# Two stacked graph layers with layer norms: column tiles one step later, and another order of work on VectorE

## The reference

```python
node = x @ W1                                   # x: 4096 x 128, W1: 128 x 16
hw   = einsum('nc,kcf->nkf', x, W2)             # W2: 16 x 128 x 128
x0   = einsum('nk,nkf->nf', node, hw)
h    = relu(adj @ x0 + node @ b)                # adj: 4096 x 4096, fp32
x1   = layernorm(x + h)                         # over the 128 features
msg  = x1 @ W + B
wts  = where(adj < 1, exp(-(1/adj - 1)**2 * 2), 0)
out  = layernorm(x1 + wts @ msg)
```

## Time and profile before

| | |
|---|---|
| median of 3 runs | 615.34 us (614.74 to 616.6) |
| profiled execution: its own time | 615.66 us |
| profiled execution: span | 613.8 us |
| TensorE busy | 570.2 us (93%) |
| ScalarE busy | 511.5 us (83%) |
| VectorE busy | 479.9 us (78%) |
| mean granted clock of TensorE | 0.982 |

### The profile page before, as it was taken

How to read it: one execution, slowest core, us unless ns; L and a number is a source line. 1 busy time by engine, 2 the same in 40 slices (tenths; PEclk the granted TensorE clock), 3 DMA queues, 4 the chain that set the end, 5 groups by cost and what they waited for, 6 DMA issues and landing times.

```text
span 613.8 us, 5199 instructions
## 1 busy us (share of the span) xinstructions
PE 570.2 (93%) x1742; PEld 322.4 (53%) x1742; DVE 479.9 (78%) x539; ACT 511.5 (83%) x542; POOL 90.2 (15%) x78
## 2 busy tenths in 40 slices
PE   6999998796899989998999899999989998988887
PEld 5888886343455545554555455545545554533332
DVE  5677778777478789879987998799789879958752
ACT  4788787859746989898989889898989898988994
POOL 1899998200000000000000000000000000000000
PEclk9999999989799999999999999999999999999989
DMA  4990000687287887787978778777887874453011
GB/s 160 361 375 18 20 0 0 230 338 288 107 304 285 308 312 280 280 321 263 336 271 338 275 280 324 289 287 287 308 310 280 280 301 186 188 205 137 18 52 68
DMA packets 22986, 142.25 MB, mean 232 GB/s; under 512 B 2704, under 2 KB 2864, under 8 KB 6576
## 3 DMA queue, kind: packets, MB, share of 16 engines
q1 hardware_dynamic: 22672, 141.65, 61.8%
q10 hardware_dynamic: 288, 0.27, 0.2%
HBM read 139.81 MB, written 2.10 MB: 231 GB/s over the span
## 4 chain that ended last, share of the span: by engine, by line
PE 53%; ACT 18%; DVE 16%; issue 8%; DMA 3%; POOL 1%; SPq 0%; POOLq 0%; ACTq 0%; DVEq 0%
PE l_ps L369 20%; PE acc_ps L334 8%; DVE wt L601 5%; PE hw_ps L306 5%; PE hw_ps L308 5%; PE hw_ps L307 5%; ACT wt L481 4%; ACT wt L469 3%; ACT wt L474 3%; ACT wt L464 3%; DVE wt L595 3%; DVE adj_lo L588 3%; DVE adj_hi L586 3%; DMA row_in<-adjT_dram 2%; PE acc_ps L327 2%
## 5 line engine op out<-in xcount | busy, mean ns | idle before, releaser
L369 PE MATMUL l_ps<-wt,msg 128*128 128x512 f32 x512 | 232.4, 597 | 12.9 <-DVE msg L632 10.9
L369 PEld LDWEIGHTS l_ps<-wt,msg 128*128 128x128 f32 x512 | 96.6, 191 | 130.9 <-issue 113.1
L595 DVE SCALAR_TENSOR_TENSOR wt<-wt 128x2048 f32<-128x2048 f32 x64 | 148.1, 2313 | 0.0
L464 ACT ACTIVATE wt<-wt 128x2048 f32<-128x2048 f32 x64 | 121.5, 1898 | 21.6 <-DVE wt L595 21.6
L334 PE MATMUL acc_ps<-row_in,x 128*128 128x512 f32 x264 | 123.1, 612 | 3.9 <-DMA row_in<-adjT_dram 3.9
L469 ACT ACTIVATE wt<-wt 128x2048 f32<-128x2048 f32 x64 | 122.4, 1912 | 2.0
L481 ACT ACTIVATE wt<-wt 128x2048 f32<-128x2048 f32 x39 | 74.3, 1905 | 40.7 <-DVE wt L601 40.7
L601 DVE SCALAR_TENSOR_TENSOR wt<-wt 128x2048 f32<-128x2048 f32 x39 | 89.1, 2284 | 8.0 <-ACT wt L469 8.0
L451 ACT ACTIVATE prods<-hw_ps,node 128x128 f32<-128x128 f32 x256 | 73.2, 373 | 18.7 <-PE hw_ps L308 17.5
L334 PEld LDWEIGHTS acc_ps<-row_in,x 128*128 128x128 f32 x264 | 51.7, 197 | 69.1 <-issue 68.9
L568 DVE SCALAR_TENSOR_TENSOR part_acc<-hw_ps,node,part_acc 128x128 f32<-128x128 f32 x224 | 60.7, 342 | 19.8 <-PE hw_ps L308 19.8
(11 more groups left out here) (63 smaller groups left out, 383.0 us busy)
## 6 DMA issues: line engine op xcount, KB each, us to landing
row_in<-adjT_dram SPq DMA_DIRECT2D x64, 1024.0 KB, 6.8
wt<-adjT_dram SPq DMA_DIRECT2D x64, 1024.0 KB, 4.8
x_in<-xT_dram SPq DMA_DIRECT2D x8, 256.0 KB, 3.6
x_row<-xT_dram SPq DMA_DIRECT2D x8, 256.0 KB, 6.1
outT_dram<-sumT SPq DMA_DIRECT2D x8, 256.0 KB, 2.0
W_in<-W_dram SPq DMA_DIRECT2D x3, 256.0 KB, 4.7
W_in<-W_dram ACTq DMA_DIRECT2D x1, 256.0 KB, 4.0
B_sb<-B_dram SPq DMA_DIRECT2D x1, 256.0 KB, 5.2
```

The lines of the kernel that those rows point to most:

```text
L369: mm = pe.matmul(l1_ps[:, t % L1_BANKS, :], msg[:, c % 2, k, :], wt[t % WT_RING][:, k, :], start=(k == 0), stop=(k == CH - 1))
L464: act.activation(w[:, :, :], w[:, :, :], ACT.Ln, bias=TINY).then_inc(ln_made, 1)
L595: dve.scalar_tensor_tensor(out=w, in0=w, scalar=1.0, in1=w, op0=ALU.is_lt, op1=ALU.mult).then_inc(mask_made, 1)
```

## The change

`COL_LAG` goes from 12 to 13: column tile t is worked at step t + 13, and its logarithm, mask, square and sum each move one step with it. `messages`, `copy_messages`, `scale_row` and `add_row` move one place too, while the row's square and inverse root on ScalarE stay. The first six weight tiles' logarithms stand at steps 0, 3, 5, 7, 10, 12 in place of 0, 2, 4, 6, 8, 10. `W1b` is made within block 1 of stage one, in a corner of a bank that the node products use, and copied after `sum_over_k(1)`. Weight tiles 6 and 7 are loaded at steps 3 and 4 of SP's loop. Within a step VectorE does: residual or copy of messages, scale, add, add of the row, square, mask, split; before it was residual or copy, add, split, mask, scale and add of the row, square. The second norm has three banks for its centred values and one for its variances, in place of two and two.

```diff
-COL_LAG = 12
+COL_LAG = 13
-FIRST_EVEN = 6
-LAST_EVEN = 58
-LAST_STEPS = (66, 67, 69, 70, 72, 73)
+FIRST_STEPS = (0, 3, 5, 7, 10, 12)
+FIRST_EVEN = len(FIRST_STEPS)
+LAST_STEPS = (67, 68, 69, 71, 72, 73)
+LAST_EVEN = 64 - len(LAST_STEPS)
...
-            return 2 * m
+            return FIRST_STEPS[m]
...
-        w1b_ps = var_ps[:, 0:P]
+        w1b_ps = acc_ps[:, 1, P:2 * P]
...
-        yc2_ps = [acc_ps[:, j % 2, :] if j < NB - 2 else l1_ps[:, j % 2, :] for j in range(NB)]
-        var2_ps = [yc_ps, var_ps]
+        yc2_ps = [(acc_ps[:, 0, :], acc_ps[:, 1, :], yc_ps[:, :])[j % 3] if j < NB - 2 else l1_ps[:, j % 2, :]
+                  for j in range(NB)]
...
-            sp.wait_ge(sum_step, NB * STEPS)
-            sp.wait_ge(fold_step, NB * FOLDS)
-            for t in range(WT_RING - LATE_SLOTS, WT_RING):
-                load_wt(t)
-
             for i in range(TILES + COL_LAG):
                 if i % NB == 1 and i // NB + 1 < NB:
                     load_x_row(i // NB + 1)
                 if i + ROW_RING < TILES:
                     load_row_tile(i + ROW_RING)
+                if i == 3:
+
+                    sp.wait_ge(sum_step, NB * STEPS)
+                    sp.wait_ge(fold_step, NB * FOLDS)
+                if 3 <= i < 3 + LATE_SLOTS:
+                    load_wt(WT_RING - LATE_SLOTS + i - 3)
...
+                if g == 3:
+
+                    pe.wait_ge(w1b_copied, 1)
...
+                    if n == GROUPS // 2 and g == 1:
+                        pe.wait_ge(const_in, CONSTS)
+                        pe.matmul(w1b_ps, W1T_sb[:, :], b0_sb[:, :], start=True, stop=True).then_inc(w1b_made, 1)
...
-                if r == 0:
-                    pe.wait_ge(w1b_copied, 1)
...
-                    at_least(pe, out_made, j - 1)
+                    at_least(pe, out_made, j - 2)
...
-                at_least(pe, ln_var2_made, j - 1)
+                at_least(pe, ln_var2_made, j)
...
-            pe.wait_ge(const_in, CONSTS)
-            pe.wait_ge(sum_step, NB * STEPS)
-            pe.wait_ge(prods_made, NB * GROUPS)
-            pe.matmul(w1b_ps, W1T_sb[:, :], b0_sb[:, :], start=True, stop=True).then_inc(w1b_made, 1)
...
-                if g == 3 and 1 <= r <= NB:
+                if g == 4 and 1 <= r <= NB:
                     messages(r - 1)
...
                 sum_over_k(g)
+                if g == 1:
+                    dve.wait_ge(w1b_made, 1)
+                    dve.tensor_copy(W1b[:, :], w1b_ps).then_inc(w1b_copied, 1)
...
-                if g == 4 and 1 <= r <= NB:
+                if g == 5 and 1 <= r <= NB:
                     copy_messages(r - 1)
+                if g == 3 and 1 <= r <= NB:
+                    scale_row(r - 1)
                 if 0 <= i - COL_LAG - 1 < TILES:
                     add_part(i - COL_LAG - 1)
-                if i + SPLIT_LEAD < TILES and is_split(i + SPLIT_LEAD):
-
-                    while remainders and remainders[0] <= (i + SPLIT_LEAD if i + SPLIT_LEAD < NB else NB):
-                        remainder_of_x0(remainders.pop(0))
-                    split_row_tile(i + SPLIT_LEAD)
-                for t in masks_at.get(i, []):
-                    mask(t)
-                if g == 2 and 1 <= r <= NB:
-                    scale_row(r - 1)
+                if g == 3 and 1 <= r <= NB:
                     add_row(r - 1)
                 for t in exps_at.get(i - 1, []):
                     if on_dve(t):
                         take_square(t)
+                for t in masks_at.get(i, []):
+                    mask(t)
+                if i + SPLIT_LEAD < TILES and is_split(i + SPLIT_LEAD):
+
+                    while remainders and remainders[0] <= (i + SPLIT_LEAD if i + SPLIT_LEAD < NB else NB):
+                        remainder_of_x0(remainders.pop(0))
+                    split_row_tile(i + SPLIT_LEAD)
```

More of the change, by code:

```diff
@@ L381, in variance2 @@
                 pe.wait_ge(sq2_made, j + 1)
-                at_least(pe, ln_var2_made, j - 1)
-                pe.matmul(var2_ps[j % 2][:, :], mean_w[:, :], sq[:, j % 2, :], start=True,
+                at_least(pe, ln_var2_made, j)
+                pe.matmul(var_ps[:, :], mean_w[:, :], sq[:, j % 2, :], start=True,
                           stop=True).then_inc(var2_made, 1)
@@ L505, in inverse_root2 @@
                 at_least(act, out_made, j - 1)
-                act.activation(rstd[:, j % 2, :], var2_ps[j % 2][:, :], ACT.Ln, bias=EPS).then_inc(ln_var2_made, 1)
+                act.activation(rstd[:, j % 2, :], var_ps[:, :], ACT.Ln, bias=EPS).then_inc(ln_var2_made, 1)
                 act.wait_ge(ln_var2_made, j + 1)
@@ L625, in last_part @@
             def last_part(r):
-                return max(t for t in range(r, TILES, NB) if t + COL_LAG + 1 <= NB * (r + 1) + 2)
+                return max(t for t in range(r, TILES, NB) if t + COL_LAG + 1 <= NB * (r + 1) + 3)
             def copy_messages(r):
@@ L640, in add_part @@
                 at_least(dve, sum_added, t - NB + 1)
-                if NB * (j + 1) + 2 < t + COL_LAG + 1:
+                if NB * (j + 1) + 3 < t + COL_LAG + 1:
                     dve.wait_ge(x1_added, j + 1)
@@ L669, in _ @@
             mask(0)
-            dve.wait_ge(w1b_made, 1)
-            dve.tensor_copy(W1b[:, :], w1b_ps).then_inc(w1b_copied, 1)
             remainders = [g for g in SPLIT]
@@ L677, in _ @@
                     residual(r - 1)
-                if g == 4 and 1 <= r <= NB:
+                if g == 5 and 1 <= r <= NB:
                     copy_messages(r - 1)
+                if g == 3 and 1 <= r <= NB:
+                    scale_row(r - 1)
                 if 0 <= i - COL_LAG - 1 < TILES:
                     add_part(i - COL_LAG - 1)
+                if g == 3 and 1 <= r <= NB:
+                    add_row(r - 1)
+                for t in exps_at.get(i - 1, []):
+                    if on_dve(t):
+                        take_square(t)
+                for t in masks_at.get(i, []):
+                    mask(t)
                 if i + SPLIT_LEAD < TILES and is_split(i + SPLIT_LEAD):
```

## The result

| | before | after |
|---|---|---|
| median | 615.33 us (614.74 to 616.6, 4 runs) | 587.74 us (586.65 to 588.17, 4 runs) |
| ratio | | 0.9546, 95% interval 0.9526 to 0.9567 |
| profiled execution: its own time, span | 615.66, 613.8 us | 586.65, 584.8 us |
| step 14, step 64 of TensorE | 179.9, 539.3 us | 160.1, 508.3 us |
| from step 64 to the end | 74.5 us | 76.5 us |

The kernel is 27.6 us faster; 585.0 us was forecast, within 578 to 596. The profiled execution of the changed kernel happens to be the fastest of its four, 1.1 us under their median.

What follows compares the result with a forecast made beforehand. TensorE was taken to pace the rows, losing time to the message copy and at both ends. Span 613.8 - 21.1 - 11.0 + 1.6 = 583.3 us gave a median of 585.0 us, range 578 to 596.

Steps and rivals of the forecast that it cites:

- What bounds the kernel: Stage two: TensorE paces the rows, and other engines' waits count only through its 10.9 us of waits for the message copy.
- The rows: Stage two, step 14 to step 64: no new wait, a row of 55.7 us for 57.5, -11.0 us in all.
- No mask waits for a DMA: Odd steps' masks in stage two come 3.5 us earlier; their tiles still land in time; a mask waiting would show the forecast wrong.
- The start: Start of stage two: earlier row tile 4 and first square bring step 14 to 158.8 from 179.9, -21.1 us.
- W1b's pair: Pair of 16-row matmuls inside stage one: 0.25 us of TensorE taken, between zero and 0.86.
- alone brings nothing: Start of stage two: row tiles starting 1.75 us earlier gain nothing alone, as split tile 3 needs VectorE's low half.
- The end: From step 64 on: one column tile more and several waits, 76.1 us for 74.5, +1.6 us, bounds 70 and 82.
- The one-bank price: Very end: the one bank of variances adds a wait on the logarithm, 0.5 to 1 us.
- The sum: Whole kernel: 613.8 - 21.1 - 11.0 + 1.6 = 583.3 us of span, 585.0 us as a median.
- The clock rival: Start and tail: each short stall left is followed by a slow group, three more give about 591 us; chance 0.08.

Runs made afterwards that it cites:

- late tiles: Changed kernel with SP's old order: weight tiles 6 and 7 wait for the last fold, ahead of every load of the loop; 594.62 us, ratio 0.9666.
- first steps: Changed kernel with the first logarithms back at steps 0, 2, 4, 6, 8, 10; 596.46 us, ratio 0.9704.
- W1b after stage one: Changed kernel with W1b made once stage one is over, in its old bank, as before; 590.51 us, ratio 0.9596.
- last copy early: Changed kernel with the last copy of messages one place earlier in VectorE's order, ahead of a square and a mask; 584.72 us, ratio 0.9509.

## Why the prediction was right, point by point

**What bounds the kernel**: right. TensorE paces the rows, and the removal of one wait of 1.6 us, with the restart behind it, shortened the row by 1.8.

**The rows, -11.0 us**: right, and in the places that were walked. From step 14 to step 64 are 508.34 - 160.10 = 348.2 us, where 348.4 was forecast (its own addends make 348.2). In the row from 341.2 on, the message copy starts 33.7 and ends 34.4 us into it, as forecast; VectorE in that row:

```profile
360.65 0.69 DVE L615 TENSOR_TENSOR y<-yc_ps,rstd 128x512 f32<-128x512 f32 x1
...
374.90 0.69 DVE L633 TENSOR_TENSOR msg<-var_ps,B_sb 128x512 f32<-128x512 f32 x1
```

No mask waits for a DMA. What the prediction left open is which part does it: the runs show that order and lag each do it alone.

**The start, -21.1 us**: -19.8, step 14 at 160.1 for 158.8. The mechanism is the one named (late tiles 6.4 us, first steps 8.3, each by a run), and the size was off by the start of one chain. What sets step 14 is ScalarE's way to the first square, and its tile 1 starts at 118.85, not 117.6:

```profile
118.85 1.92 ACT L465 ACTIVATE wt<-wt 128x2048 f32<-128x2048 f32 x1 [0.62 <-DVE wt L596]
```

From there on its 1.2 us is carried to the variance (142.4 for 141.2) and to step 14. The prediction moved TensorE's row tiles and left VectorE's and ScalarE's work where it had been, but the 16 products of stage one, which these two follow, end later as well: W1b's pair cost 0.6 us in place of 0.25, between its bounds (from one node product to the next are 12.45 us with it, 11.84 without), and the clock rises 1.1 us later within its first matmuls than it did before, which costs another 0.5. The second is chance: in twelve executions of this same stage one it ends between 102.87 and 104.70 us, here at 104.16, and 103.5 was forecast.

The first `centre` waits 1.49 us, not 0.3, since VectorE stood 2.52 us before row tile 9's load. That costs nothing, for the variance then waits 0.47 in place of 2.3. That W1b's move "alone brings nothing" isn't borne out: undone, it costs 1.8 us by step 14, by the clock behind a longer wait, and 2.3 or more in the medians.

**The end, +1.6 us**: +2.0, which is in part luck. The single terms were near: the wait for the last copy is 4.41 (4.7 forecast), the slow stretch behind it 1.5 us (1.8), the square's wait 1.42 (1.6), `scale_row`'s 0.88 (1.2). But the prediction's terms don't make its sum: 60.9 + 1.6 + 1.2 + 4.7, 2 to 3 among the last variances and 0.5 to 1 for the logarithm are 70.9 to 72.4, not 69.9, and the whole term would have been +2.6 to +4.1. It comes out because the 2 to 3 us among the last variances weren't there: all that TensorE waits for behind the last copy is 0.53 and 0.78 us for the logarithm (0.5 to 1 forecast). The one-bank price was seen as a cost; the run with the old banks shows that the third bank for centred values is worth more.

**The sum**: 583.3 us of span forecast, 584.8 found. The median lies a further 1.1 us above the profiled time, while before it lay 0.3 under it. The four executions differ in their granted clocks too (0.990 to 0.995). The clock rival has a slow stretch behind the wait at the first split tile. The profiled execution doesn't have it, but two others with the same program up to its last rows do, and their first variance comes 0.8 and 1.1 us later, counted from the first row tile. That the slower three of the four are such is likely, not shown.

## What to carry to other kernels

Where one engine paces the loop, write down its step starts and walk the others against them once. Each wait of the others is free up to its slack, and here waits of 40 us and 33 us hid one wait of 1.6 us per row that cost something.

When a wait is a queue's fault, move the late item behind what is wanted sooner: one wait for stage one's last fold, ahead of loads that didn't need it, cost 6 us.

To price a wait, look for the next one behind it. A wait that a later one takes in is free (the old first steps' wait at the split tile, the changed kernel's at `centre`); the same wait right ahead of the step that bounds the stretch isn't (W1b after stage one).

And don't read 1 us off one trace each: the same stretch of the same program differed by that much from one execution to the next.

## What the runs showed of the hardware

The lower clock after a short wait is not certain. In ten executions TensorE waited 2.14 or 2.15 us for the same low half. In six of them the clock fell behind it, in four it didn't, also where the program up to there was the same. The mean granted clock from 116 to 140 us (the third number from the end of the row) was 1.00 in the changed kernel run again and 0.93 in the one with the last copy early:

```profile
116.00:140.00 24.00, 21.33 (x67) 12.40 (x68) 21.51 (x14) 23.09 (x13) 0.00 (x0) 1.00 0.94 372
```

```profile
116.00:140.00 24.00, 22.35 (x65) 13.39 (x66) 19.92 (x13) 23.09 (x13) 0.00 (x0) 0.93 0.90 360
```

In the second most of the split tile behind the wait ran at 0.43 us a matmul, not 0.23, and the tile took 1.5 us more. The two kinds differ in when the wait came: it ended at 116.63 us or later in the four, at 116.48 or earlier in the six. Behind the 4.41 us of idle before the last message block, the clock fell each time, but not for equally long: the sixteen matmuls took 8.56, 8.56, 8.83, 9.47, 9.72, 9.93, 10.04 and 10.04 us in eight executions, 7.03 at full clock. The Trainium skill's page "TensorE: Matmul & The Clock Gate" (section "Why this matters for your kernels") warns of idle gaps between bursts; the runs agree for the gaps of 2.95 and 4.41 us shown above, and show that one of 2.15 us goes either way. The warning is of long gaps, so the 1.55 us that the prediction set against it doesn't contradict the page.

VectorE's first mask of stage two took 4.32 us, its others 2.28, and the three fold passes that GpSimd ran in that time 6.76 us in place of 4.58:

```profile
105.76 4.32 DVE L596 SCALAR_TENSOR_TENSOR wt<-wt 128x2048 f32<-128x2048 f32 x1
```

```profile
100.14 4.58 POOL L713 TENSOR_TENSOR prods<-prods 128x1024 f32<-128x1024 f32 x3
...
105.58 6.76 POOL L713 TENSOR_TENSOR prods<-prods 128x1024 f32<-128x1024 f32 x3 [0.32 <-ACT prods L452]
```

Each lost about 2 us: GpSimd 2.2, about one mask (2.28), VectorE 2.0, somewhat more than one fold pass (1.5). The Trainium skill's page "SBUF — State Buffer" (section "SBUF: two separate sides") describes the port pair that the two share as held for a whole instruction; the rows fit that loosely. It isn't shown as the cause: no run here moved the mask out of the folds' way.
